# A mixture-of-experts layer on one core: the router's weights turned ahead of the last early unit, one semaphore per stored chunk, and two late turns moved five units back

## The reference, cut to what matters

```python
x = x + _L1_ffn_ref(_layernorm(x), ...)          # lf, and again as lh
# inside, with T = 2048 tokens, E = 32 experts, L = 16 anchors:
scores = sigmoid(x @ gate_weight.T)
sc = scores + gate_bias
# two of four expert groups, six experts in them, weights normalised to 0.2
cw = (one_hot(topidx, E) * tw[..., None]).sum(1)              # T x E
routed = einsum('te,teh->th', cw, (silu(x @ w_gate_e) * (x @ w_up_e)) @ w_down_e)
shared = silu(x @ shared_w_gate) * (x @ shared_w_up) @ shared_w_down
acw = one_hot(topidx[:, 0] // 2, L)                           # T x L
out = routed + shared + 0.1 * einsum('tl,tlh->th', acw, anchor experts of x)
```

## Time and profile before

| | |
|---|---|
| three runs | 1726.14, 1726.68, 1727.53 us; median 1726.68 |
| the profiled execution | 1724.85 us, its span 1723.1 us |
| mean granted TensorE clock | 0.91 |
| busy over the span | PE 81%, DVE 71%, ACT 42%, POOL 41% |
| layer lf, last matmuls of it included | about 1095 to 1307 us |
| layer lh | about 1507 to the end |

### The profile page before, as it was taken

The page is one execution under the profiler, slowest core; times in us unless marked ns, Lnnn a source line. Parts: engine busy times, 40 slices in busy tenths (PEclk is TensorE's granted clock), DMA queues, the critical chain, the costliest instruction groups (busy, mean ns, idle before and its releaser), DMA issues. The chain is left out here.

```text
span 1723.1 us, 26589 instructions
## 1 busy us (share of the span) xinstructions
PE 1400.1 (81%) x9106; PEld 942.8 (55%) x9106; DVE 1218.5 (71%) x2920; ACT 729.0 (42%) x1224; POOL 706.2 (41%) x905
## 2 busy tenths in 40 slices
PE   4799999939996549977588899889996387489998
PEld 3333333326874328853466566667884177367786
DVE  5777777374555675556799899678777744669776
ACT  2276767621214112136544343355554411154554
POOL 3824241027622137600366566036664051006665
PEclk9599999969998769989799999899998699689999
DMA  1144230000100001100000000444440000065443
GB/s 41 61 126 131 79 137 2 1 25 25 34 16 12 25 0 38 37 18 1 0 1 1 1 1 1 180 118 117 136 132 17 0 1 1 1 216 129 134 133 105
DMA packets 73239, 96.21 MB, mean 56 GB/s; under 512 B 24656, under 2 KB 42592, under 8 KB 72608
## 3 DMA queue, kind: packets, MB, share of 16 engines
q1 hardware_dynamic: 73120, 94.71, 18.9%
HBM read 84.42 MB, written 10.26 MB: 55 GB/s over the span
## 5 line engine op out<-in xcount | busy, mean ns | idle before, releaser
L526 DVE CUSTOM_DVE_ANT_1 la_neg<-bank,la_table 128x512 f32<-128x512 f32 x256 | 166.3, 688 | 44.8 <-PE bank L617 44.2
L1656 POOL TENSOR_TENSOR lh_h_low<-lh_hidden,lh_h_high 128x512 fp32r<-128x512 f32 x84 | 111.4, 1328 | 161.5 <-ACT lh_h_high L1689 161.2
L1454 PEld LDWEIGHTS bank<-le_diag,le_dtxT 128*128 128x128 f32 x1024 | 126.5, 191 | 80.5 <-issue 59.0
L1454 PE MATMUL bank<-le_diag,le_dtxT 128*128 128x128 f32 x1024 | 142.0, 282 | 25.4 <-DVE le_h L1372 21.3
L1372 DVE TENSOR_TENSOR_SCAN le_h<-le_keep,bank 128x512 f32<-128x512 f32 x128 | 155.2, 1213 | 3.8 <-PE bank L1454 3.8
L1656 POOL TENSOR_TENSOR lf_h_low<-lf_hidden,lf_h_high 128x512 fp32r<-128x512 f32 x84 | 111.5, 1329 | 109.1 <-ACT lf_h_high L1689 108.8
L1310 ACT ACTIVATE le_keep<-le_dt,le_A 128x512 f32<-128x512 f32 x128 | 92.1, 722 | 133.1 <-DVE le_h L1372 133.1
L453 ACT ACTIVATE la_probT<-bank 128x512 f32<-128x512 f32 x256 | 135.6, 605 | 12.9 <-PE bank L636 10.9
L1225 POOL TENSOR_TENSOR le_hc<-le_hc 128x512 f32<-128x512 f32 x64 | 81.0, 1266 | 101.4 <-DVE le_hc L1381 97.6
L1679 ACT ACTIVATE bank<-bank 128x512 f32<-128x512 f32 x144 | 83.7, 581 | 62.0 <-PE bank L1844 60.3
L1233 POOL TENSOR_TENSOR le_diag<-ident,le_bT 128x512 f32<-128x512 f32 x64 | 71.3, 1136 | 71.3 <-ACT le_bT L1297 70.3
(11 more groups left out here) (568 smaller groups left out, 3534.3 us busy)
## 6 DMA issues: line engine op xcount, KB each, us to landing
lf_weight<-lf_scratch SPq DMA_DIRECT2D x128, 128.0 KB, 3.0
lh_weight<-lh_scratch SPq DMA_DIRECT2D x128, 128.0 KB, 3.0
la_table<-la_scratch SPq DMA_DIRECT2D x4, 1792.0 KB, 7.3
lf_weight<-lf_scratch SPq DMA_DIRECT2D x64, 64.0 KB, 2.2
lh_weight<-lh_scratch SPq DMA_DIRECT2D x64, 64.0 KB, 2.2
la_bias_parts<-la_scratch_parts SPq DMA_DIRECT2D x12, 248.0 KB, 6.3
lb_w1s<-in_L_ffn_w_dram SPq DMA_DIRECT2D x8, 256.0 KB, 2.8
lb_w2s<-in_L_ffn_w_dram SPq DMA_DIRECT2D x8, 256.0 KB, 3.1
```

Of the source, the lines that this page charges most:

```text
L526: dve.tensor_tensor_reduce(out=neg[:, u % 2, :].rearrange("p (c i) -> p c i", i=P), in0=k.bank[u % RING1][:].rearrange("p (c i) -> p c i", ...
L1454: last = pe.matmul(k.bank[4 + q % 2][:, j * P:(j + 1) * P], dtxT[:, (g * G2 + bb) * TPB + j, c, :], diag[:, d % DIAGS, j, :], start=True, ...
L1656: pool.tensor_tensor(h_low[:, u % RING, :], hidden[:, u % RING, :], h_high[:, u % RING, :].bitcast(F32), ALU.subtract)\
```

## The change

Five edits, all in `layer_moe_tokens`, so all of them twice in the program:

1. PE turns chunks 0 and 1 of the stack in front of the last of the 12 early units, and ACT copies them behind the copies of the last early unit but one.
2. Each chunk's store has a semaphore of its own, and a chunk's first load waits for that chunk's store alone. Before, the first load of chunk 0 waited for the stores of chunks 0 and 1, the first load of chunk 2 for all four.
3. `SECOND_TURNS` moves from units 30 and 33 to 35 and 38, `SECOND_DUE` from 29 to 34.
4. PE does ten idle products into bank 7 behind the products of unit 2.
5. The waits for the first two copies that stood in front of the down product of unit 0 and of the first chunk's turned sum stand in front of those idle products.

```diff
-        stack_ready, stack_turned, stackT_ready, stackT_stored = sem("stack_ready"), sem("stack_turned"), sem("stackT_ready"), sem("stackT_stored")
+        stack_ready, stack_turned, stackT_ready = sem("stack_ready"), sem("stack_turned"), sem("stackT_ready")
+        stackT_stored = [sem(f"stackT_stored{c}") for c in range(B)]
...
-        SECOND_TURNS = {TILES + 9: 2, TILES + 12: 3}
-        SECOND_DUE = TILES + 8
+        SECOND_TURNS = {TILES + 14: 2, TILES + 17: 3}
+        SECOND_DUE = TILES + 13
...
             def store(c):
                 at = slice(c * T, (c + 1) * T)
                 sp.wait_ge(stackT_ready, c + 1)
-                sp.dma_start(scratch[:, at], stackT[:, at]).then_inc(stackT_stored, 16)
+                sp.dma_start(scratch[:, at], stackT[:, at]).then_inc(stackT_stored[c], 16)
...
-                if u == 0:
-                    sp.wait_ge(stackT_stored, 32)
-                if u == 2 * TILES:
-                    sp.wait_ge(stackT_stored, 64)
+                if s == 0:
+                    sp.wait_ge(stackT_stored[c], 16)
...
                 act.activation(up_e[:, i, c * T:(c + 1) * T], k.bank[GB + n % GB][:], ACT.Copy).then_inc(early_kept, 1)
+                if n == EARLY * B - 2:
+                    for half in range(2):
+                        copy_stackT(half)
...
-            for c in range(2):
-                copy_stackT(c)
             for u in range(LAG):
                 silu(u)
...
             for n in range(EARLY * B):
                 i, c = n // B, n % B
+                if n == EARLY * B - 1:
+                    turn_stack(0)
+                    turn_stack(1)
                 if n >= GB:
                     pe.wait_ge(early_kept, n - GB + 1)
...
                 if u == 0:
                     pe.wait_ge(loaded_down, 32)
...
                     pe.wait_ge(stackT_ready, B)
-                else:
-                    pe.wait_ge(stackT_ready, 2)
...
-            turn_stack(0)
-            turn_stack(1)
             for u in range(U):
                 products(u)
+                if u == LAG - 1:
+                    pe.wait_ge(stackT_ready, 2)
+                    k.idle_products(pe, 10, 7)
                 if u >= LAG:
                     down(u - LAG)
```

More of the change, by code:

```diff
@@ L1660, in _, with copy_stackT @@
         def _(act):
+            def copy_stackT(c):
+                act.wait_ge(stack_turned, c + 1)
+                act.activation(stackT[:, c * T:(c + 1) * T], k.bank[6 + c % 2 if c < 2 else 7][0:STK, :], ACT.Copy).then_inc(stackT_ready, 1)
             norm.scalar_sqrt(act)
@@ L1679, in silu @@
                 act.activation(k.bank[v % GB][:], k.bank[v % GB][:], ACT.Silu).then_inc(silu_ready, 1)
-            def copy_stackT(c):
-                act.wait_ge(stack_turned, c + 1)
-                act.activation(stackT[:, c * T:(c + 1) * T], k.bank[6 + c % 2 if c < 2 else 7][0:STK, :], ACT.Copy).then_inc(stackT_ready, 1)
             def round_hidden(u):
@@ L1844, in gate_up, with turn_stack @@
                 return pe.matmul(bank[:], low[:, w], x_high[:, x], start=False, stop=True)
+            def turn_stack(c):
+                bank = k.bank[6 + c % 2 if c < 2 else 7]
+                pe.wait_ge(stack_ready, c // 2 + 1)
+                if c == 2:
+                    pe.wait_ge(acc_used, 1)
+                if c == 3:
+                    pe.wait_ge(stackT_ready, 3)
+                for j in range(TPB):
+                    last = pe.transpose(bank[0:STK, j * P:(j + 1) * P], stack[:, c * TPB + j, :], k.ident[:])
+                last.then_inc(stack_turned, 1)
             pe.wait_ge(loaded_gw, 16)
@@ L1880, in products @@
                     gate_up(k.bank[GB + v % GB], wu_high, wu_low, t, c).then_inc(up_done, 1)
[L1882 to L1891, removed]
             def down(u):
```

## The result

The changed kernel is slower: 1735.82 us median of 9 runs against 1727.0 of 9 runs of the kernel before; the ratio is 1.0049, with a 95% interval of 1.0029 to 1.0068, or +5.0 to +11.7 us. One of the nine runs of the kernel before was slow, at 2830.51 us, and the ratio leaves it out. Forecast were +6.6 us, and for eight in ten 1728.0 to 1737.0. The span of the profiled execution is 1736.9 us (before 1723.1). Part of that difference lies in code that the change doesn't touch: ahead of lf 1099.1 us against 1097.2, in the layer between lf and lh 200.5 against 199.8.

The account below looks back on a forecast made before the run. DVE was taken to set the pace in units 0 to 22, PE later. Start −3.6, stall +8.0 and clock +2.2 gave +6.6 us on 1726.7: 1733.3 us, own range 1730.5 to 1736.5, eight in ten 1728.0 to 1737.0.

Parts of the forecast that it names:

- start: Start of each token layer: first weights 1.74 us sooner in lf, 1.85 in lh, 3.6 us gained in all.
- late turns, stall: At unit 38: SP's held queue delays the weights, PE loses 4.0 us a layer, 8.0 in all.
- late turns, clock: Behind PE's stop at unit 38: a clock fall costs 1.5 us, three of four: 1.1 a layer, 2.2 in all.
- What is pushed back: At the layer's start: the last early unit and its two ACT copies come behind the turn, at no cost.
- the idle products: Ten on PE behind unit 2: 2.2 to 4.4 us filling a gap, cost and gain taken as 0.
- near 0.5 in the following 3 us: Sign to look for: granted clock near 0.5 for 3 us behind PE's 3 us idle near unit 38.
- DVE carries this to unit 23: Units 0 to 23: the start's gain moves everything behind it, since DVE waited for the load and is busy afterwards.
- only the start counts: Rival: unit 38's weights land in time, late turns are free, −3.6 us remains, 1723.1 us; chance 0.06.
- Late turns cost half: Rival: DVE closes up behind unit 38's stall, about 2 us a layer remain, +0.4 us, 1727.1; chance 0.11.
- the clock stays up: Rival: the stall at unit 38 is there but no clock fall follows, +4.4 us, 1731.1; chance 0.15.
- the idle products hurt: Rival: clock falls before unit 0, unit 3 comes some 3 us late a layer, +12.6 us, 1739.3; chance 0.06.

## Why the prediction was right, and where it was off

| term, us for both layers | forecast | measured |
|---|---|---|
| start (from the waits below) | −3.6 | −3.9 |
| late turns, stall | +8.0 | +8.2 |
| late turns, clock | +2.2 | +2.1 |
| clock between the first two chunks | none | +2.7 |
| sum | +6.6 | +9.1 (time: +5.0 to +11.7) |

*The start.* Where the routing ends 28.8 to 29.1 us behind the layer's start, the wait for the first weights is 9.12 to 9.26 us without the early start and 6.80 to 7.26 with it; where it ends at 30.4 to 30.7, 10.36 to 10.57 and 8.36 to 9.43. On the mean of each kind that is 2.2 and 1.8 a layer, some 1.95 over all, against the 1.74 and 1.85 of the forecast; the turn has 1.3 to 1.6 of it (1.26 to 1.37 were expected), the semaphore 0.6 to 0.7 (0.48).

*What is pushed back, and the idle products.* Both were put at nothing, and units 0 to 23 are 49.3 and 49.7 us in the changed kernel against 49.1 to 49.7 in the kernel before, so neither costs much. The wait at unit 6 in lf with idle products, up to 1.95 us, was not foreseen.

*The late turns.* The working held from link to link. Unit 27 of lf comes 2.75 us later in the profile after than before (1196.81 against 1194.06); with that added the forecast has the copy of chunk 3 at 1218.95 (measured 1218.69), the multiply of unit 38 at 1223.65 (1223.40), the start of PE's stop at 1222.65 (1222.41 + 0.23) and the last matmul of the down product at 1227.05 to 1227.55 (1226.89). The stall of 4.0 a layer is 4.09 with the clock held up. The clock's 1.1 against 1.06 is in part luck: the forecast was a price of 1.5 us at a chance of three in four, while the clock fell behind the stop in all four layers with late turns and nothing in the stop, at 1.06 us on average. The sign "near 0.5 in the following 3 us" came as 0.76 and 0.67 in two stretches of 3 us. It is SP's queue, as forecast, and nothing else: with the stores on another queue the cost is gone.

*Where it was off.* The start's gain was carried to the end undiminished: "DVE carries this to unit 23", and behind it no loss was looked for. The stop between the first two chunks stood in the earlier trace rows with one fall in two, and I took it to be the same before and after. With both halves of the early start the clock falls there every time, in place of one layer in eight, which takes 1.57 us of the 1.95 back: 2.7 for the two layers (14 of 14 against 1 of 8). So of the start by itself, which the rival "only the start counts" put at −3.6, −1.2 us remain by the terms, a ratio of 0.9993. The four kernels with it and without the late turns' loss measured 0.9997, 1.0004, 1.0005 and 1.0007; the interval of the last begins at 0.9995, so the true rest may be smaller, as the wait at unit 6 would make it. The time of the changed kernel, +5.0 to +11.7, cannot tell the forecast's +6.6 from the +9.1 of the terms: the missing 2.7 us is read from the traces, and the range was wide enough to hold it. The forecast's own range of 1730.5 to 1736.5 is also not the one that its ends make (3.2 to 5.0 a layer for the stall, 0 to 3 for the clock): that is 1729.5 to 1736.1.

*The rivals.* "Late turns cost half" fell with 4.09 us of stall; "the clock stays up" with 0.67 to 0.76 granted behind it; "the idle products hurt", which asked for some 3 us a layer, with the 49.3 and 49.7 us of units 0 to 23.

## What to carry to other kernels

A producer that is moved later costs at the queue that stores it: look for what stands in that queue behind the store, for any other consumer, before looking at the engines that do the moved work. Here five units' delay was free on PE and ACT, free with the store on a queue of its own, free at three units fewer, and 5.15 us a layer in front of someone else's loads. And a gain ahead of a stop of the engine that sets the pace is only had if the clock behind that stop stays up: idle products in a stop that is there anyway turned a start that gave nothing measurable into 0.29%.

## What the runs showed of the hardware that was not expected

- The same stop of 2.5 us brought the clock down to half in 17 of 26 layers, not at random by kernel: 1 of 8, 2 of 4, 14 of 14. Among the 19 layers in which the clock last rose 68 to 72 us before, the distance from that rise sorts them without exception (69.2 us and less fell, 69.8 to 70.7 not, 71.5 fell). What a stop of this length does in one profile says little of what it does in a neighbour of that kernel.
- Idle products of 2.1 us in the stop of 2.5 kept the clock at 1.00 in both layers, and so did 2.76 us of them at unit 38, with a rest of 0.64 us unfilled.
- Code that no edit touches, ahead of lf, took 1093.6 to 1101.4 us in these profiles. So two profiles can differ there by 7.8 us, nearly as much as the change does; the sections that PE sets repeat to 0.1 us where no stop falls in them (units 46 to 82: 68.74 or 68.75 in every one; 27 to 46: 36.30 to 36.38 without the stall), while units 0 to 23 range from 49.1 to 50.1 where no stop was put into them.
